# First attention of a four-stage kernel: the division of its outputs goes from VectorE to ScalarE, VectorE and GpSimd, and 44 of 64 row maxima stand ahead of the second scores, not 56

## The chip, the cores and the metric

The kernel runs on one core of one Trainium2 chip. The metric is the device time of one execution in microseconds, the median of several runs. A core has TensorE (matrix products, PE in the rows), VectorE (DVE), ScalarE (ACT), GpSimd (POOL) and SyncE (SP, which only issues transfers here). Each engine takes its instructions in the order in which they are written and waits at semaphores for the others. TensorE writes its products to PSUM, which has eight banks of 512 float32 values in each of 128 partitions.

## The reference, cut to what matters

```python
x = L0_attn_x                                    # (8, 512, 128), 16 heads of 8
x = _layernorm(x + _L0_attn_ref(x, L0_attn_W_qkv), axis=-1)
x = _layernorm(x + _L0_ffn_ref(x, ...), axis=-1)   # mixture of 32 experts and a shared one
x = _layernorm(x + _L1_attn_ref(x, ...), axis=-1)
x = _layernorm(x + _L1_ffn_ref(x, ...), axis=-1)
...
qkv = x @ W_qkv                                   # _L0_attn_ref
q, k, v = jnp.split(qkv, 3, axis=-1)
...
scores = jnp.einsum('bhnd,bhmd->bhnm', q, k) / jnp.sqrt(jnp.float32(D_MODEL))
attn = jax.nn.softmax(scores, axis=-1)
out = jnp.einsum('bhnm,bhmd->bhnd', attn, v)
```

The change touches the first attention alone, and the places in its last stretch where the work of the expert stage begins.

## The kernel before

`attention0` works through the eight batch items. An item has 16 heads and four tiles of 128 queries, so 64 **first scores**: products of bfloat16 parts of the queries with the keys (`s1`, L627), each 128 by 512 in one bank of `ps_f`. VectorE takes the negated maximum of every row of each (`reduce_max`, L780). The maxima go back into the product: half an item at a time GpSimd splits them into three bfloat16 parts (`split_max`), TensorE turns the parts (`turn_max`, L601), ScalarE copies them out of PSUM (`take_max`, L502), and SyncE writes them as extra rows into the operand `qs` (`max_rows`, L453). The **second scores** (`s2`, L683, 64 products in 32 units `u` of two) then come out of TensorE with the maximum subtracted and the keys in the partitions; ScalarE takes their exponential (L542), and TensorE multiplies by the values (`pv`, L696, one group of four column tiles for every two units). ScalarE takes the summed outputs of eight heads (`take_o`), TensorE turns them (`turn_o`, L704), and VectorE divides them by the sum that stands in an extra column (`divide`, L791 and L229). GpSimd adds x and normalises.

The stages of neighbouring items overlap. While the 32 units of second scores of item b run (a **period** below), the remaining first scores of item b and the first ones of item b+1 are interleaved, two to a unit, at 64 **turns** 0 to 63: turns below `LATE` belong to item b, the others to item b+1. Four **guests** have a turn of their own: the two turned maxima `max0`, `max1` and the two turned outputs `o0`, `o1`. Turn n stands in unit n // 2; in an odd unit a `pv` group stands between the first turn and the second. The order of a unit on TensorE is: second scores, first turn, `pv` if the unit is odd, second turn.

```python
GUEST_AT = {"max0": MT_AT[0], "max1": MT_AT[1],
            "o0": OT_AT[0], "o1": OT_AT[1]}
TURNS = [t for n in range(S1_N) for t in [g for g, at in GUEST_AT.items() if at == n] + [n]]
BANK = {t: i % FB for i, t in enumerate(TURNS)}
```

First scores and guests go round three PSUM banks (`FB = 3`) in this order. Before a turn writes, `free_bank` waits until the turn three places back in `TURNS` has been read: a score by its maximum, a turned maximum by ScalarE's copy, a turned output by the division. So a guest takes one place in the round of three. The second scores have a pair of double banks of their own, the outputs one bank.

Ahead of period 0 stands a **lead** (`units(-1, ...)`): the first scores of item 0 from turn `LATE` on, two a unit, with no second scores. From unit `EARLY_U` on each unit of it has one of 22 `early_product`s (L614, L617) in float32, which ScalarE copies (`take_early`); units without one have three products that only keep TensorE at work (`warm_up`, L592). The second scores of item 0 wait for the last copy. SyncE's queue is written out in `step`. Between the lead and period 0's transfers stand the weights of the later stages (`load_more`), and its end waits until all of the small ones have landed. GpSimd's order stands in its own `units`; `split_qk` (L292 to L304) makes the bfloat16 parts of the item after next, which SyncE writes out and reads back as `qs` and `ks` (`parts_to_dram`, `stack`). In the last period `Front` begins the routing of the experts: for seven items TensorE turns x (L950) and, two units later, multiplies it by the gate (L942), at the units `X_AT0`.

## Time and profile before

| | us |
|---|---|
| median of 3 runs | 1024.18 (1024.17 to 1026.49) |
| the profiled execution, its own time | 1023.77 |
| its span, first to last instruction | 1021.7 |
| TensorE, VectorE, ScalarE, GpSimd busy in the span | 979.9, 826.8, 732.8, 523.6 |
| from the start to the first second scores (the lead) | 51.5 |
| a period of 32 units in the middle of the first attention | 41.6 |

Times within the span are counted from its first instruction. Busy time of TensorE counts pipelined products that overlap, so 96% of the span is not 96% of what it can do. The first attention fills the span up to about 386 us.

### The profile page before, as it was taken

What the parts mean: (1) busy time and instruction counts of PE and PEld (TensorE: products, weight loads), DVE (VectorE), ACT (ScalarE), POOL (GpSimd) and SP (SyncE); (2) the same over time, 40 slices, a digit from 0 to 9 for tenths busy, and PEclk for the clock granted to TensorE, in tenths of its full rate; (3) what the DMA queues carried; (4) which work ended last, traced back from release to release, by engine and by line L of the source; (5) the groups of instructions that cost most, each with busy time, mean ns of one, the idle gap of its engine ahead of it and who ended that gap; (6) DMA issues with size and microseconds to landing.
All of it is one profiled execution on the core that took longest, in us unless ns stands there. A gap on an engine that the chain in (4) does not pass through costs nothing. (4 is left out here: it accounts for less than half of the span.)

```text
span 1021.7 us, 20122 instructions
## 1 busy us (share of the span) xinstructions
PE 979.9 (96%) x5769; PEld 469.4 (46%) x5769; DVE 826.8 (81%) x1811; ACT 732.8 (72%) x945; POOL 523.6 (51%) x631
## 2 busy tenths in 40 slices
PE   8999999999999999999999999999999999999996
PEld 4422222222222246888888887863232333222585
DVE  7999999999999867889788789987666666644677
ACT  4377887878888776655555555668889888999753
POOL 3051744726538745677677676675443144310275
PEclk9999999999999999999999999999999999999999
DMA  7661223122130005323433432443422332230011
GB/s 229 205 226 48 81 64 109 45 87 95 40 109 17 3 4 165 122 87 127 143 99 95 154 115 80 151 147 98 150 87 68 92 123 73 66 108 1 1 32 52
DMA packets 73548, 97.04 MB, mean 95 GB/s; under 512 B 12620, under 2 KB 42188, under 8 KB 73100
## 3 DMA queue, kind: packets, MB, share of 16 engines
q1 hardware_dynamic: 73496, 96.40, 29.7%
q8 instruction: 26, 0.43, 0.2%
q14 instruction: 26, 0.21, 0.1%
HBM read 68.18 MB, written 27.79 MB: 94 GB/s over the span
## 5 line engine op out<-in xcount | busy, mean ns | idle before, releaser
L780 DVE TENSOR_REDUCE a_nmax<-a_ps_f 128x1 f32<-128x512 f32 x512 | 319.7, 683 | 7.7 <-PE a_ps_f L627 5.3
L542 ACT ACTIVATE a_prob<-a_ps_s 128x1024 f32<-128x1024 f32 x256 | 250.0, 1022 | 63.5 <-PE a_ps_s L683 62.3
L1428 ACT ACTIVATE a_prob<-a_ps_s 128x1024 f32<-128x1024 f32 x256 | 244.4, 1026 | 27.8 <-PE a_ps_s L1480 26.8
L2248 POOL TENSOR_TENSOR moe_hl<-moe_hid,moe_hh 128x512 fp32r<-128x512 f32 x134 | 174.2, 1305 | 84.1 <-ACT moe_hh L2129 84.0
L627 PE MATMUL a_ps_f<-a_ks,a_qs 48*128 48x512 bf16 x512 | 156.9, 384 | 10.7 <-DVE a_nmax L780 3.1
L2119 ACT ACTIVATE moe_ps<-moe_ps 128x512 f32<-128x512 f32 x128 | 74.5, 582 | 111.6 <-PE moe_ps L2042 110.8
L1493 PE MATMUL a_ps_o<-a_prob,a_va 128*32 128x512 f32 x1024 | 136.4, 605 | 1.8 <-DVE a_turned_o L1608 1.2
L696 PE MATMUL a_ps_o<-a_prob,a_va 128*32 128x512 f32 x1024 | 136.4, 605 | 0.5 <-ACT a_prob L542 0.4
L683 PE MATMUL a_ps_s<-a_qs,a_ks 51*128 51x512 bf16 x512 | 131.8, 381 | 1.7 <-ACT a_prob L542 1.4
L627 PEld LDWEIGHTS a_ps_f<-a_ks,a_qs 48*128 48x128 bf16 x512 | 38.5, 93 | 193.9 <-DVE a_nmax L780 188.1
L2170 DVE TENSOR_TENSOR moe_prod<-moe_cw,moe_ps 128x512 f32<-128x512 f32 x128 | 87.3, 682 | 27.4 <-PE moe_ps L2042 26.7
L1480 PE MATMUL a_ps_s<-a_qs,a_ks 48*128 48x512 bf16 x512 | 91.0, 384 | 11.2 <-ACT a_prob L1428 10.0
L2179 DVE TENSOR_TENSOR moe_hid<-moe_prod,moe_ps 128x512 f32<-128x512 f32 x128 | 86.9, 679 | 6.1 <-DVE moe_prod L2170 1.9
L2129 ACT ACTIVATE moe_hh<-moe_hid 128x512 fp32r<-128x512 f32 x136 | 84.8, 624 | 6.1 <-DVE moe_hid L2179 5.9
L1480 PEld LDWEIGHTS a_ps_s<-a_qs,a_ks 48*128 48x128 bf16 x512 | 23.1, 93 | 129.1 <-ACT a_prob L1428 104.7
L838 POOL TENSOR_TENSOR a_msplit<-a_nmax,g_zero 128x32 bf16<-128x32 f32 x16 | 3.8, 239 | 142.7 <-DVE a_nmax L780 142.7
L2040 PE MATMUL moe_ps<-moe_xh,moe_whig 128*128 (+1 forms) x136 | 55.0, 405 | 1.3 <-DVE moe_hid L2179 1.3
L2067 PE MATMUL moe_ps<-moe_hl,moe_whid 128*128 128x512 f32 x136 | 53.9, 397 | 0.9 <-POOL moe_hl L2248 0.9
L2040 PE MATMUL moe_ps<-moe_xh,moe_whiu 128*128 (+1 forms) x136 | 53.8, 395 | 0.0
L2062 PE MATMUL moe_ps<-moe_hh,moe_wlod 128*128 128x512 f32 x136 | 53.7, 395 | 0.0
L2041 PE MATMUL moe_ps<-moe_xh,moe_wlog 128*128 (+1 forms) x136 | 53.7, 395 | 0.0
L2061 PE MATMUL moe_ps<-moe_hh,moe_whid 128*128 128x512 f32 x136 | 53.6, 394 | 0.0
(324 smaller groups left out, 1636.1 us busy)
## 6 DMA issues: line engine op xcount, KB each, us to landing
moe_cw<-r_weights SPq DMA_DIRECT2D x256, 128.0 KB, 2.8
parts_q<-a_parts SPq DMA_DIRECT2D x48, 256.0 KB, 2.5
parts_k<-a_parts SPq DMA_DIRECT2D x48, 256.0 KB, 2.6
a_qs<-parts_q SPq DMA_DIRECT2D x126, 96.0 KB, 2.4
a_ks<-parts_k SPq DMA_DIRECT2D x126, 96.0 KB, 2.4
out_x<-g_X SPq DMA_DIRECT2D x7, 256.0 KB, 2.3
a_prob<-in_x_t SPq DMA_DIRECT2D x3, 512.0 KB, 5.4
moe_wg<-in_wg SPq DMA_DIRECT2D x1, 1088.0 KB, 6.7
```

Source lines behind the costliest of these rows:

```text
L542: nc.scalar.activation(prob[:, u % PSLOTS, :, :], ps_s[:, u % 2, :, :], ACT.Exp, scale=float(P) ** -0.5).then_inc(exp_done, 1)
L627: nc.tensor.matmul(ps_f[:, bank, :], stack_rows(qs[p], h, QKR)[:, qt * P:(qt + 1) * P], stack_rows(ks[p], h, QKR), start=True, stop=True). ...
L683: mm = nc.tensor.matmul(ps_s[:, u % 2, i, :], stack_rows(ks[p], h, MXR)[:, kt * P:(kt + 1) * P], stack_rows(qs[p], h, MXR), start=True, st ...
L696: mm = nc.tensor.matmul(ps_o[j * CT:(j + 1) * CT, :], v_of_head(va[p], kt, grp * HG + j), prob[:, (2 * e + j // UN) % PSLOTS, j % UN, :], ...
L780: nc.vector.tensor_reduce(nmax[:, half_no, h % 2, col:col + 1], ps_f[:, bank, :], AX.X, ALU.max, negate=True).then_inc(max_done, 1)
L1428: nc.scalar.activation(prob[:, u % PSLOTS, :, :], ps_s[:, u % 2, :, :], ACT.Sigmoid, scale=float(HD) ** -0.5).then_inc(exp_done, 1)
L1480: mm = nc.tensor.matmul(ps_s[:, u % 2, i, :], stack_rows(ks[p], h, QKR)[:, kt * P:(kt + 1) * P], stack_rows(qs[p], h, QKR), start=True, st ...
L1493: mm = nc.tensor.matmul(ps_o[j * CT:(j + 1) * CT, :], v_of_head(va[p], kt, grp * HG + j), prob[:, (2 * e + j // UN) % PSLOTS, j % UN, :], ...
L2040: nc.tensor.matmul(dst, w[0][:, j, :], hi, start=True, stop=False)
L2170: nc.vector.tensor_tensor(prod[:, bank(j), :], cw[:, slot(j), :], ps_u[:, bank(j), :], ALU.mult).then_inc(prod_done, 1)
L2179: nc.vector.tensor_tensor(hid[:, hid_at(j), :], prod[:, bank(j), :], ps_g[:, bank(j), :], ALU.mult).then_inc(hid_done, 1)
L2248: nc.gpsimd.tensor_tensor(hl[:, part_at(j), :], hid[:, hid_at(j), :], hh[:, part_at(j), :], ALU.subtract).then_inc(hl_done, 1)
```

## The change

`LATE` goes from 8 to 20: the lead has 44 turns, and 20 of the 64 first scores of an item stand in its own period. The early products begin at unit 10, where the lead's first turn now is. The two turned maxima move from turns 47 and 11 to 58 and 24. For all items but the last, ScalarE copies a turned output from PSUM to `turned_o` in SBUF (`take_turned`), which frees the bank; VectorE takes the reciprocal of the sums from there at turn 50 or 13 (`invert`), and GpSimd multiplies (`divide`). GpSimd's `split_qk` moves behind the split of the maxima and behind this multiplication, SyncE's `parts_to_dram` behind `max_rows`. In the last period, turning x for the router begins at unit 13 and routing at unit 18, where they began at 7 and 14.

```diff
--- before.py
+++ after.py
@@ -51,7 +51,7 @@
 WEIGHT_SCALE = 1.0 / 127.0
 S1_N = H * NT
 FB = 3
-LATE = 8
+LATE = 20
 WARM = (5, 2, 3)
 PLACED = 2
 RC, CW_EARLY = 8, 3
@@ -60,11 +60,12 @@
 HH = H // 2
 V_AT = 16
 EARLY = [("q", 1), ("k", 1), ("v", 0), ("v", 1)] + [(name, b) for b in range(2, NB) for name in "qkv"]
-EARLY_U = 5
+EARLY_U = 10
 EARLY_BANKS = 4
-MT_AT = (47, 11)
+MT_AT = (58, 24)
 OT_AT = (46, 9)
 STATS_AT = 16
+REC_AT = (50, 13)
 LOOP_U = 11
 
 
@@ -348,6 +349,7 @@
         osb = [sb("osb0", [P, T]), e["dsb"]]
         sel = prob[:, PSLOTS - 1, :, :].rearrange("p i t -> p (i t)").bitcast(BF16)[:, 0:2 * PARTS * PLACED * (HALF + QKR)]
         sel = sel.rearrange("p (n a j m) -> p n a j m", n=2, a=PARTS, j=PLACED)
+        turned_o = sb("turned_o", [P, T])
         pool_gate, qk_gate = sb("pool_gate", [P, 1]), sb("qk_gate", [P, 4])
         squares, half_sums, sums, share = sb("squares", [P, NT, P]), sb("half_sums", [P, NT, P // 2]), sb("sums", [P, NT]), sb(
             "share", [P, NT])
@@ -376,6 +378,7 @@
         s2_done, exp_done, pv_done = sem("s2_done"), sem("exp_done"), sem("pv_done")
         o_taken, ot_done, rec_done, att_done, sum_done, norm_step = (
             sem(n) for n in ("o_taken", "ot_done", "rec_done", "att_done", "sum_done", "norm_step"))
+        o_copied = sem("o_copied")
 
 
         S2_C, EXP_C, PV_C, O_C, OT_C, ATT_C = NU, 2, PSLOTS // 2, 1, 2, 1
@@ -458,11 +461,10 @@
                     max_rows(b, p, 1)
                 if fore and back:
                     stack(b + 1, 1 - p, NG - 1, True)
-                if qk_on:
-                    parts_to_dram(b + 2, p)
                 if fore:
                     max_rows(b + 1, 1 - p, 0)
                 if qk_on:
+                    parts_to_dram(b + 2, p)
                     sp.wait_ge(parts_out, OUT_C * (b + 3) + OUT_C)
                     for grp in range(NG - 1):
                         stack(b + 2, p, grp, True)
@@ -526,6 +528,11 @@
                 act.wait_ge(ot_done, NO * b + n - 1 + OT_C)
                 take(osb[n][:, :], ps_o[:, :], pv_done, NE * b + PER_O * NT * (n + 1) + PV_C, o_taken)
 
+            def take_turned(b, n):
+
+                act.wait_ge(att_done, NO * b + n + ATT_C)
+                take(turned_o[:, :], ps_f[:, BANK[f"o{n}"], :], ot_done, NO * b + n + 1 + OT_C, o_copied)
+
             def take_max(b, half_no):
 
                 k = 2 * b + half_no
@@ -547,6 +554,10 @@
                         for t in turns_of(u, second):
                             if fore and back and t == V_AT and not is_first(b):
                                 place_v(b + 1, 1 - p)
+                            if back and t == "o0" and not is_last(b):
+                                take_turned(b, 0)
+                            if tail and t == "o1" and not is_last(b):
+                                take_turned(b - 1, 1)
                             if fore and t == "max0":
                                 take_max(b + 1, 0)
                             if back and t == "max1":
@@ -638,7 +649,11 @@
                 elif t in ("max0", "max1"):
                     pe.wait_ge(mt_copied, 2 * b + (t == "max0"))
                 else:
-                    pe.wait_ge(att_done, NO * (b - 1) + (int(t[1]) + 1) % NO + ATT_C)
+                    count = NO * (b - 1) + (int(t[1]) + 1) % NO
+                    if is_last(b - 1):
+                        pe.wait_ge(att_done, count + ATT_C)
+                    else:
+                        pe.wait_ge(o_copied, count)
 
             def take_turn(b, p, t, qk_on, fore, back, tail):
 
@@ -780,6 +795,12 @@
                 nc.vector.tensor_reduce(nmax[:, half_no, h % 2, col:col + 1], ps_f[:, bank, :], AX.X, ALU.max,
                                         negate=True).then_inc(max_done, 1)
 
+            def invert(b, n):
+
+                dve.wait_ge(o_copied, NO * b + n + 1)
+                dve.wait_ge(att_done, NO * b + n + ATT_C)
+                nc.vector.reciprocal(rec[:, :, :, :], output_parts(turned_o[:, :])[:, :, :, :, HD]).then_inc(rec_done, 1)
+
             def divide(b, n):
 
                 o = output_parts(ps_f[:, out_bank(b, n), :])
@@ -796,10 +817,14 @@
                 for u in range(u0, u1):
                     for second in range(2):
                         for t in turns_of(u, second):
-                            if back and t == "o0":
+                            if back and t == "o0" and is_last(b):
                                 divide(b, 0)
-                            if tail and t == "o1":
+                            if tail and t == "o1" and is_last(b):
                                 divide(b - 1, 1)
+                            if back and t == REC_AT[0] and not is_last(b):
+                                invert(b, 0)
+                            if tail and t == REC_AT[1] and not is_last(b):
+                                invert(b - 1, 1)
                             if isinstance(t, int) and (back if t < LATE else fore):
                                 reduce_max(*score_of(t, b), BANK[t])
                     if is_last(b):
@@ -843,6 +868,15 @@
                 pool.wait_ge(mt_chain, 3 * k + 3)
                 nc.gpsimd.tensor_tensor(msplit[:, :, 2, :], mrest[:, :, :], msplit[:, :, 1, :],
                                         ALU.subtract).then_inc(mt_parts, 1)
+
+            def divide(b, n):
+
+                o, to = output_parts(turned_o[:, :]), outputs_of(att, n)
+                pool.wait_ge(rec_done, NO * b + n + 1)
+                for q in range(PER_O):
+                    ins = nc.gpsimd.tensor_tensor(to[:, :, :, q, :], o[:, :, :, q, 0:HD],
+                                                  rec[:, :, :, q].unsqueeze(3).broadcast_to([P, NT, HG, HD]), ALU.mult)
+                ins.then_inc(att_done, 1)
 
             def add_x(b):
 
@@ -891,9 +925,11 @@
                 if u0 == 0 and is_first(b):
                     front.split_weight(pool, 0)
                 if u0 == 0 and tail:
+                    if not is_last(b):
+                        divide(b - 1, 1)
                     add_x(b - 1)
                     normalise(b - 1)
-                if u1 == NU and qk_on:
+                if u1 == NU and qk_on and not back:
                     split_qk(b + 2, 0)
                     split_qk(b + 2, 1)
                 if u1 == NU and fore:
@@ -906,6 +942,11 @@
                     if isinstance(b, int) and b < 0:
                         pool.wait_ge(x_in, 16)
                         pool.wait_ge(early_taken, len(EARLY))
+                    if back:
+                        divide(b, 0)
+                    if qk_on and back:
+                        split_qk(b + 2, 0)
+                        split_qk(b + 2, 1)
                     if isinstance(b, int) and b == NB - 2:
                         front.split_weight(pool, 3)
                         front.split_weight(pool, 4)
@@ -918,9 +959,9 @@
     return FirstOutput(nc, g, e, m, o_taken, osb[1], rec, att, ln, ot_done, rec_done, att_done, sum_done)
 
 
-X_AT0 = (7, 9, 11, 13, 21, 23, 25)
+X_AT0 = (13, 15, 17, 19, 21, 23, 25)
 X_POOL = (4, 5, 6)
-EXP_AT, ROUTE_U, CT_U = 13, 14, 23
+EXP_AT, ROUTE_U, CT_U = 18, 18, 23
 NEXT_ROUTE_AT = (26, 28, 28, 28, 29, 29, 29, 30, 30, 30, 31, 31)
 ROUTE_PER_U = 2
 
```

The order on TensorE in the first half of the loop's body, from the second scores of unit 23 on. `a_ps_s` are second scores, `a_ps_f<-a_ks,a_qs` first scores, `a_ps_o` is `pv`, `a_ps_f<-g_ident,a_osb` the guest `o0` and `a_ps_f<-a_identb,a_msplit` the guest `max0`. Before:

```order
L683 MATMUL a_ps_s<-a_qs_76,a_ks_77 128x512 x2
L637 REGISTER_ALU
L704 MATMUL a_ps_f<-g_ident,a_osb 128x128 x4
L637 REGISTER_ALU
L627 MATMUL a_ps_f<-a_ks,a_qs 128x512
L696 MATMUL a_ps_o<-a_prob,a_va_78 32x512 x4
L637 REGISTER_ALU
L600 ISA
L601 MATMUL a_ps_f<-a_identb,a_msplit 96x128
L627 MATMUL a_ps_f<-a_ks,a_qs 128x512
```

And now, the same place with `o0`, then unit 29 with `max0`:

```order
L698 MATMUL a_ps_s<-a_qs_76,a_ks_77 128x512 x2
L648 REGISTER_ALU
L719 MATMUL a_ps_f<-g_ident,a_osb 128x128 x4
L648 REGISTER_ALU
L638 MATMUL a_ps_f<-a_ks,a_qs 128x512
L711 MATMUL a_ps_o<-a_prob,a_va_78 32x512 x4
L648 REGISTER_ALU
L638 MATMUL a_ps_f<-a_ks,a_qs 128x512
...
L698 MATMUL a_ps_s<-a_qs_76,a_ks_77 128x512 x2
L648 REGISTER_ALU
L611 REGISTER_ALU
L612 MATMUL a_ps_f<-a_identb,a_msplit 96x128
L648 REGISTER_ALU
L638 MATMUL a_ps_f<-a_ks,a_qs 128x512
L711 MATMUL a_ps_o<-a_prob,a_va_78 32x512 x4
```

`o0` stays where it is. `max0` stood behind the `pv` of the same unit; now it stands in another unit, ahead of the first turn and of `pv`.

The order on TensorE around `max1`. Before, where it stands in unit 5, behind `o1` in unit 4:

```order
L704 MATMUL a_ps_f<-g_ident,moe_dsb 128x128 x4
L627 MATMUL a_ps_f<-a_ks_77,a_qs_76 128x512
L680 REGISTER_ALU
L683 MATMUL a_ps_s<-a_qs,a_ks 128x512 x2
L637 REGISTER_ALU
L627 MATMUL a_ps_f<-a_ks_77,a_qs_76 128x512
L696 MATMUL a_ps_o<-a_prob,a_va 32x512 x4
L600 REGISTER_ALU
L601 MATMUL a_ps_f<-a_identb,a_msplit 96x128
```

And now, in unit 12:

```order
L698 MATMUL a_ps_s<-a_qs,a_ks 128x512 x2
L648 REGISTER_ALU
L611 REGISTER_ALU
L612 MATMUL a_ps_f<-a_identb,a_msplit 96x128
L648 REGISTER_ALU
L638 MATMUL a_ps_f<-a_ks_77,a_qs_76 128x512
L648 REGISTER_ALU
L638 MATMUL a_ps_f<-a_ks_77,a_qs_76 128x512
L695 REGISTER_ALU
L698 MATMUL a_ps_s<-a_qs,a_ks 128x512 x2
L650 REGISTER_ALU
L638 MATMUL a_ps_f<-a_ks_77,a_qs_76 128x512
```

It stands alone now, three first scores ahead of the next `pv`, and the first score behind the next unit's second scores has its bank.

On VectorE the division in the first half of the body was, and is now:

```order
L780 TENSOR_REDUCE a_nmax<-a_ps_f 128x1
L786 REGISTER_ALU
L788 REGISTER_ALU
L791 RECIPROCAL a_rec<-a_ps_f 128x32
L229 TENSOR_TENSOR moe_y<-a_ps_f,a_rec 128x4x32 x2
```

```order
L795 TENSOR_REDUCE a_nmax<-a_ps_f 128x1
L800 REGISTER_ALU
L802 RECIPROCAL a_rec<-a_turned_o 128x32
L794 REGISTER_ALU
L795 TENSOR_REDUCE a_nmax<-a_ps_f 128x1
```

The two multiplications are gone from VectorE, and the reciprocal stands four maxima later.

## Rows read from the trace of the kernel before

**Rows 1.** The page: busy time of each engine.

```profile
PE 979.9 (96%) x5769; PEld 469.4 (46%) x5769; DVE 826.8 (81%) x1811; ACT 732.8 (72%) x945; POOL 523.6 (51%) x631
```

**Rows 2.** One period: length; busy PE, PEld, DVE, ACT, POOL; clock, DMA share, GB/s.

```profile
176.70:218.30 41.60, 40.21 (x266) 10.11 (x266) 41.17 (x71) 33.28 (x38) 22.14 (x43) 1.00 0.25 77
```

**Rows 3.** Waits, 176.7 to 260 us: in total, times, longest.

```profile
PEld a_ps_f L627 <- DVE a_nmax L780: 48.9, 89, 0.8
...
DVE a_nmax L780 <- PE a_ps_f L627: 0.6, 2, 0.3
```

**Rows 4.** Timeline of VectorE: start, length; maxima 1, 4 and 5 of five.

```profile
210.44 0.69 DVE L780 TENSOR_REDUCE a_nmax<-a_ps_f 128x1 f32<-128x512 f32 x1
...
212.24 0.68 DVE L780 TENSOR_REDUCE a_nmax<-a_ps_f 128x1 f32<-128x512 f32 x1
...
212.93 0.69 DVE L780 TENSOR_REDUCE a_nmax<-a_ps_f 128x1 f32<-128x512 f32 x1
```

**Rows 5.** Timeline of TensorE in the same two units.

```profile
211.18 0.09 PEld L627 LDWEIGHTS a_ps_f<-a_ks,a_qs 48*128 48x128 bf16 x1 [0.51 <-DVE a_nmax L780]
...
211.50 1.07 PE L696 MATMUL a_ps_o<-a_prob,a_va 128*32 128x512 f32 x8
...
212.50 0.39 PE L627 MATMUL a_ps_f<-a_ks,a_qs 48*128 48x512 bf16 x1
```

**Rows 6.** Timeline around `o0`: TensorE, VectorE; two exponentials of ScalarE.

```profile
205.42 0.66 PE L704 MATMUL a_ps_f<-g_ident,a_osb 128*128 128x128 f32 x4
...
206.48 0.35 DVE L791 RECIPROCAL a_rec<-a_ps_f 128x32 f32<-128x32 f32 x1
206.86 0.49 DVE L229 TENSOR_TENSOR moe_y<-a_ps_f,a_rec 128x128 f32<-128x128 f32 x2
207.26 11.93 DVE L780 TENSOR_REDUCE a_nmax<-a_ps_f 128x1 f32<-128x512 f32 x19
...
213.22 1.94 ACT L542 ACTIVATE a_prob<-a_ps_s 128x1024 f32<-128x1024 f32 x2 [0.55 <-PE a_ps_s L683]
```

**Rows 7.** Timeline of VectorE at a period's start.

```profile
179.02 3.77 DVE L780 TENSOR_REDUCE a_nmax<-a_ps_f 128x1 f32<-128x512 f32 x6 [0.30 <-PE a_ps_f L627]
```

**Rows 8.** Timeline of the lead: TensorE; last early copy on ScalarE.

```profile
13.01 0.82 PE L592 MATMUL a_ps_o<-a_identb 128*128 128x512 bf16 x3
...
14.85 1.13 PE L617 MATMUL a_ps_s<-a_xt,a_w 128*128 128x512 f32 x2
...
45.78 0.60 ACT L520 ACTIVATE a_early_v<-a_ps_s 128x512 f32<-128x512 f32 x1 [0.81 <-PE a_ps_s L614]
...
51.51 0.39 PE L683 MATMUL a_ps_s<-a_qs,a_ks 51*128 51x512 bf16 x2
```

**Rows 9.** Timeline of period 0: copy and transfer of maxima; next period's first exponential.

```profile
59.44 0.27 ACT L502 ACTIVATE a_mparts<-a_ps_f 96x128 bf16<-96x128 bf16 x1 [0.60 <-PE a_ps_f L601]
...
64.49 1.49 SPq L453 DMA_DIRECT2D a_qs<-a_mparts  x2
...
93.11 1.02 ACT L542 ACTIVATE a_prob<-a_ps_s 128x1024 f32<-128x1024 f32 x1 [0.55 <-PE a_ps_s L683]
```

**Rows 10.** DMA issues on the page: median us to landing.

```profile
a_qs<-parts_q SPq DMA_DIRECT2D x126, 96.0 KB, 2.4
```

**Rows 11.** Timeline of TensorE in the last period: second scores of units 8, 10, 28.

```profile
352.52 0.70 PE L683 MATMUL a_ps_s<-a_qs,a_ks 51*128 51x512 bf16 x4
...
355.62 0.61 PE L683 MATMUL a_ps_s<-a_qs,a_ks 51*128 51x512 bf16 x4
...
380.43 0.61 PE L683 MATMUL a_ps_s<-a_qs,a_ks 51*128 51x512 bf16 x4
```

**Rows 12.** GpSimd by form, 176.7 to 218.3 us; timeline of GpSimd and SyncE.

```profile
L200 POOL TENSOR_TENSOR a_half_sums<-a_half_sums 128x128 f32<-128x128 f32 x2 | 0.9, 462 | 0.2
...
196.32 0.20 POOL L295 TENSOR_TENSOR a_qk_gate<-g_zero 128x1 f32<-128x1 f32 x1
...
206.15 0.87 SPq L263 DMA_DIRECT2D parts_k<-a_parts  x2
```

## The prediction

> **What bounds the kernel now.** I read the page first, for the engines: TensorE seems full and VectorE comes next [rows 1], but TensorE's records overlap, so this decides nothing. The busy times of one middle period say that VectorE is at work for 41.17 of 41.60 us [rows 2]. The waits say nearly the same from the other side: the first scores wait 48.9 us for maxima in two periods, the maxima 0.6 us for scores [rows 3]. So far VectorE is the bound, and whatever leaves it is a gain.
>
> The timeline, maximum by maximum, says something else. From 210.44 to 212.24 us three maxima start 0.60 us apart; the next starts 0.69 later [rows 4]. This fourth one is the turn behind `pv`: its score starts at 212.50 and its maximum at 212.93, 0.43 behind, which is the bare way from product to maximum. VectorE could have begun at 212.84 and waits 0.09, too little for the views to call idle. Following the chain back: the maximum that starts at 210.44 ends at 211.13, the score three places on loads its weights at 211.18, having waited for it (this is the bank), `pv` stands behind that score and starts at 211.50, and the next score can start when its 1.00 us is over, at 212.50 [rows 4, 5]. The loop is 0.69 + 0.05 + 0.32 + 1.00 + 0.43 = 2.49 us, and four turns take 2.49 us. So three PSUM banks, and `pv` in TensorE's order, set the pace; VectorE would need 4 x 0.60 = 2.41. It has 0.08 us to spare in four turns and nothing more.
>
> A rule that speaks against the change goes with this. By the Trainium skill, Perfetto Trace Analysis, section Optimization Strategy, the same small gap repeated on the engine that should be saturated can mean that there is too little PSUM for the next tile; the repeated 0.08 us is such a gap. It would put the gain of a lighter VectorE at that gap alone; my sum comes out the same way from the loop.
>
> A period of 64 turns is then 16 x 2.485 = 39.76. The two divisions with the guests beside them bring it to 41.6: a division holds VectorE from 206.48 to 207.26, 0.78 [rows 6], and the period's start idles 0.30 [rows 7]; 39.76 + 2 x 0.78 + 0.30 = 41.62.
>
> **The change, part by part.** All is counted against the profiled execution, 1023.77 us (0.4 below the median of 1024.18).
>
> *The lead.* Before, a unit with three warming products stands ahead of the first early product: they start at 13.01, the product at 14.85. Now the product takes the place at 13.01, 1.84 earlier; 22 units with a product follow as before, with one turned maximum among them. The last copy ends at 46.38 before [rows 8], so now at 44.54, and the second scores may start at 44.6 where they started at 51.51: **-6.9**. The turned maximum is no later than that: it stands two products before the end, and its transfer needs two issues of 0.75 and a landing of 2.4 [rows 9, 10], about 4.2 in all against 4.1 of products and 0.7 of copy.
>
> *A guest alone.* Here the change costs. A guest takes one place in the round of three banks. With `o0` ahead of the turn before `pv`, that turn gets the bank of the score two back instead of three, whose maximum starts one pitch later: the loop grows by 0.60. Before, this lay under the division (0.78) and `max0` stood in the same four turns, as did `max1` beside `o1`: two guests, one stall. Now the four stand in four places. `max0` at turn 58 has the same place as `o0`, ahead of the score before `pv`: +0.60. `max1` at turn 24 stands three scores ahead of `pv`; the score before `pv` gets the bank of `max1` itself, which ScalarE frees. ScalarE comes to it only behind the exponential of unit 12. That exponential starts 0.72 behind the score after `pv` (213.22 against 212.50), two take 1.94, of which the first holds ScalarE for 0.92 [rows 5, 6], and the copy takes 0.27 [rows 9]. Counted from the score after `pv`, the bank is free at 1.91, where the maximum of the score three places back would have freed it at 0.43 + 0.69 + 0.05 = 1.17. The loop grows by the 0.74 between them and by the 0.05 of a release: **0.79**. Bounds: a guest costs nothing if VectorE has scores in store (its place in the order, 0.2 of TensorE, is what would remain), and 0.78 by the division's row.
>
> *The divisions.* VectorE now does the reciprocal alone: 206.48 to 206.86, 0.38 [rows 6], less the 0.08 to spare: 0.30, at a turn of its own. The guest's 0.60 now stands bare. Together 0.90 each where a division was 0.79. ScalarE's two copies, of 0.60 each as in [rows 8], fit: in 2.49 us it has two exponentials of 1.94, and the copy lies behind the exponential and before the bank is asked for. If the cover is gone, a copy's 0.60 is paid. GpSimd's two multiplications are 0.46 each by its row of this size [rows 12], 1.0 at most.
>
> *A middle period* is then 39.76 + 2 x 0.90 + 0.79 + 0.60 + 0.30 = 43.25, against 41.64: +1.61, six times: **+9.7**.
>
> *Period 0.* From the second scores to those of period 1 it was 93.11 - 0.72 - 51.51 = 40.9 [rows 8, 9]. Now, without `o1`: 39.76 + 0.90 + 0.79 + 0.60, less 0.5 since there is no `pv` in the first cycle: 41.5, **+0.6**. And a new wait. The maxima of the second half are copied at 59.7 but their transfer is issued at 64.49 [rows 9], since SyncE waits for the weights of later stages to land. That was hidden: unit 16, the first to need them, came half a period after 51.51, near 72. Now it is due eight cycles after 44.6, less 0.5 and with the 0.79 of `max1`, at 64.8. The weights are queued behind the lead's turned maximum, which comes 1.84 earlier by the start and 1.4 later by one more product; I take them 0.5 earlier. The transfer then begins at about 64.0, its second half at 64.75, and by the 2.4 of a transfer eight times as large [rows 10] it lands at 67.1 at the latest; I take 66.6. TensorE stands in front of unit 16 with the first scores behind it: **+1.8** (bounds 0, if the weights land 2 us earlier, and 2.3).
>
> *The queues.* GpSimd's order: `split_max` for turn 51, the division, then `split_qk`, from 196.32 until SyncE writes its last part at 206.15, 9.8 us [rows 12]. Maxima are ready about 36 us into a period, so the parts are ready at 48.2, that is 4.9 in the next; written (three issues of 0.44 and a landing of 2.4, 3.7) and read back (four issues, 3.8 with the landing of the last) [rows 10, 12] by 12.4, where the first score of the item is due at 13.9. A margin of 1.5 us, with the multiplications at 1.0 still 0.4. Cost nothing.
>
> *The last period.* Units 0 to 9 now have first scores, so unit 10 comes 0.4 later (a single guest's 0.60 less what the older order lost). Before, two clusters of turned x stood in it; a pair of units with one takes 355.62 - 352.52 = 3.10, about 3.0 with the next ones. From unit 10 to unit 28 it was 24.8 [rows 11]. Now unit 10 to 14 has little (2 x 1.94 of exponentials at least, 4.6 with a turned maximum and a turned x), then come seven pairs of 3.0 to 3.1, `o0` adding 0.6, one of them: 4.6 + 7 x 3.06 + 0.6 = 26.6. +1.8 and +0.4, and 0.3 for routing that starts closer to its exponential: **+2.5**.
>
> Sum: -6.9 + 9.7 + 0.6 + 1.8 + 2.5 = +7.7, so **1031.5 us**. Its own range, by guests at 0.45 to 0.8 (27 places): 1027 to 1035.
>
> **The rivals.** A measurement of this kernel can tell about 0.3%, 3.1 us, from no change.
>
> *VectorE is the bound after all.* 41.17 of 41.60 us busy [rows 2] speak for it, the 0.69 step in every fourth place [rows 4] against it. Then a guest costs nothing, each of 13 divisions saves 0.78 - 0.38 = 0.40, together 5.2, the lead 6.9, and the last period and unit 16 take back 2.5 and 1.8: 1016.0, **faster**. It decides if the guests cost less than 0.1 each. The Trainium skill states the rule behind it, Perfetto Trace Analysis, Identifying the Most-Contended Engine: for VectorE occupancy is a fair measure, and the engine with the highest is to be optimised first. Chance 0.25.
>
> *Guests cost half.* Scores stored in other banks hide part: 27 places of 0.25 less give about 1025. Chance 0.10.
>
> *The parts of the next item come late.* If writing and reading back take over 1.5 us more than in rows 10, each later microsecond is paid in six periods: 1 us late is 1037. Chance 0.06.
>
> My forecast has 0.59, of which 0.04 lies within 0.3%.
>
> **The numbers.** Faster 0.25, within 0.3% 0.13, slower 0.62. The range reaches from 1015 to 1036; below it a part of the first rival is left out, above it the third.
>
> **What the profile of the changed kernel would show.** The first second scores at about 44.6. A middle period of 43.2. Steps of 1.2 to 1.3 us from one maximum to the next, with idle of 0.5 to 0.7 put down to the first scores, at turns 11, 27, 47 and 59, and none before. A transfer of maxima at about 64 in period 0 with TensorE idle until 66.5. No wait of first scores for parts. I am wrong if the four turns with a guest alone take 2.5 us, or if a middle period is below 41.6.

## The result, and the profile after

The changed kernel takes **1031.11 us** (median of 4 runs, 1030.48 to 1031.7), the kernel before 1024.3 us beside it: a ratio of 1.0056, with an interval of 1.0036 to 1.0075. It is slower by 6.8 us, where +7.7 was forecast; the time itself lies 0.4 us from the forecast and inside its range. The profiled execution took 1030.48 us, its span is 1028.6.

One middle period, which answers to [rows 2], with the same columns:

```profile
174.48:217.36 42.88, 40.79 (x268) 10.53 (x268) 40.20 (x68) 33.89 (x39) 23.68 (x48) 1.00 0.23 75
```

It is longer by 1.28 us while VectorE works 0.97 us less in it. What stands in its way shows in the waits from 174.48 to 260.24 us (two periods, as in [rows 3]; total, times, longest):

```profile
PEld a_ps_f L638 <- DVE a_nmax L795: 47.5, 80, 0.8
...
DVE a_nmax L795 <- PE a_ps_f L638: 5.3, 10, 0.6
```

The maxima waited 0.6 us for scores, now 5.3. The page has the same for the whole span: the group of the maxima with its idle time behind the second bar, before and after.

```profile
L780 DVE TENSOR_REDUCE a_nmax<-a_ps_f 128x1 f32<-128x512 f32 x512 | 319.7, 683 | 7.7 <-PE a_ps_f L627 5.3
```

```profile
L795 DVE TENSOR_REDUCE a_nmax<-a_ps_f 128x1 f32<-128x512 f32 x512 | 319.5, 683 | 25.8 <-PE a_ps_f L638 23.9
```

The timeline of VectorE in that period says where (start, length, work, count, idle before it):

```profile
182.84 1.29 DVE L795 TENSOR_REDUCE a_nmax<-a_ps_f 128x1 f32<-128x512 f32 x2 [0.60 <-PE a_ps_f L638]
184.05 0.34 DVE L802 RECIPROCAL a_rec<-a_turned_o 128x32 f32<-128x32 f32 x1
184.31 8.11 DVE L795 TENSOR_REDUCE a_nmax<-a_ps_f 128x1 f32<-128x512 f32 x13
...
193.68 12.43 DVE L795 TENSOR_REDUCE a_nmax<-a_ps_f 128x1 f32<-128x512 f32 x20 [0.62 <-PE a_ps_f L638]
206.71 1.89 DVE L795 TENSOR_REDUCE a_nmax<-a_ps_f 128x1 f32<-128x512 f32 x3 [0.60 <-PE a_ps_f L638]
208.51 0.34 DVE L802 RECIPROCAL a_rec<-a_turned_o 128x32 f32<-128x32 f32 x1
...
214.87 2.48 DVE L795 TENSOR_REDUCE a_nmax<-a_ps_f 128x1 f32<-128x512 f32 x4 [0.60 <-PE a_ps_f L638]
```

Four stops of 0.6 us: ahead of the maxima of turns 11 (182.84), 27 (193.68), 47 (206.71) and 59 (214.87). Between them stand the two reciprocals. Below I call the time from the start of the maximum of turn 4k-1 to that of turn 4k+3 **cycle** 4k+3. It takes 2.49 us where nothing disturbs it. I read the sixteen cycles of each period off VectorE's timeline, for this kernel and all that follow; each ends with the first maximum behind a `pv`. A period is counted from the maximum of one turn 63 to the next.

| us | before | after |
|---|---|---|
| cycle 3 (the period's start) | 2.79 | 2.79 |
| cycle 11, 15 (`o1`, its reciprocal) | 3.27, 2.49 | 3.08, 2.60 |
| cycle 27 (`max1` now) | 2.49 | 3.27 |
| cycle 47, 51 (`o0`, its reciprocal) | 3.28, 2.49 | 3.08, 2.61 |
| cycle 59 (`max0` now) | 2.49 | 3.08 |
| maximum of turn 63, period 0 | 92.81 | 88.71 |
| the same, period 6 | 342.86 | 346.41 |
| first product of the expert stage | 385.69 | 391.75 |

The lead gives what was asked of it. The second scores begin here (TensorE):

```profile
45.11 0.39 PE L698 MATMUL a_ps_s<-a_qs,a_ks 51*128 51x512 bf16 x2 [0.73 <-issue]
```

And the wait of unit 16 in period 0, forecast as new, is there. ScalarE has copied the maxima at 62.05, but SyncE waits for the small weights and issues them at 64.35; TensorE waits for them until 67.57. The first line is from the waits of SyncE from 38 to 70 us (L2591 is the end of `load_more`), the others from the timeline.

```profile
SPq L2591 <- DMA a_ob<-in_o_b: 6.8, 1, 6.8
...
64.35 1.50 SPq L456 DMA_DIRECT2D a_qs<-a_mparts  x2
...
67.57 0.39 PE L698 MATMUL a_ps_s<-a_qs,a_ks 51*128 51x512 bf16 x2 [1.27 <-DMA a_qs<-a_mparts]
```

Something that the forecast left out stands in period 6, where cycle 59 is 3.58. GpSimd splits two weights of the expert stage ahead of the maxima, and comes to the maxima at 340.68, 0.5 us too late for turn 58:

```profile
332.14 4.81 POOL L1074 TENSOR_TENSOR moe_wlog<-moe_wg,moe_whig 128x2176 fp32r<-128x2176 f32 x1
336.91 3.81 POOL L1071 TENSOR_TENSOR moe_whiu<-moe_wu,g_zero 128x2176 fp32r<-128x2176 f32 x1
340.68 0.23 POOL L863 TENSOR_TENSOR a_msplit<-a_nmax,g_zero 128x32 bf16<-128x32 f32 x1
```

### The profile page after: what moved, and what is told of

Read it like the earlier page. It is cut to its first block and busy times, and to the rows that moved or that the text cites. A ratio compares the mean times of both kernels' runs of the same rounds, so it can differ in the third digit from the quotient of the medians.

```text
span 1028.6 us, 20103 instructions
## 1 busy us (share of the span) xinstructions
PE 979.0 (95%) x5751; PEld 470.4 (46%) x5751; DVE 821.8 (80%) x1785; ACT 736.3 (72%) x958; POOL 534.0 (52%) x657
## 3 DMA queue, kind: packets, MB, share of 16 engines
q1 hardware_dynamic: 73496, 96.40, 29.9%
## 5 line engine op out<-in xcount | busy, mean ns | idle before, releaser
L795 DVE TENSOR_REDUCE a_nmax<-a_ps_f 128x1 f32<-128x512 f32 x512 | 319.5, 683 | 25.8 <-PE a_ps_f L638 23.9
L1469 ACT ACTIVATE a_prob<-a_ps_s 128x1024 f32<-128x1024 f32 x256 | 244.5, 1026 | 28.2 <-PE a_ps_s L1521 27.1
L2289 POOL TENSOR_TENSOR moe_hl<-moe_hid,moe_hh 128x512 fp32r<-128x512 f32 x134 | 174.4, 1306 | 84.0 <-ACT moe_hh L2170 83.9
L638 PE MATMUL a_ps_f<-a_ks,a_qs 48*128 48x512 bf16 x512 | 161.0, 384 | 13.5 <-DVE a_nmax L795 3.5
L2083 PE MATMUL moe_ps<-moe_xl,moe_whig 128*128 (+1 forms) x136 | 53.6, 394 | 0.0
```

Source lines behind the costliest of these rows:

```text
L638: nc.tensor.matmul(ps_f[:, bank, :], stack_rows(qs[p], h, QKR)[:, qt * P:(qt + 1) * P], stack_rows(ks[p], h, QKR), start=True, stop=True). ...
L795: nc.vector.tensor_reduce(nmax[:, half_no, h % 2, col:col + 1], ps_f[:, bank, :], AX.X, ALU.max, negate=True).then_inc(max_done, 1)
L1469: nc.scalar.activation(prob[:, u % PSLOTS, :, :], ps_s[:, u % 2, :, :], ACT.Sigmoid, scale=float(HD) ** -0.5).then_inc(exp_done, 1)
L2289: nc.gpsimd.tensor_tensor(hl[:, part_at(j), :], hid[:, hid_at(j), :], hh[:, part_at(j), :], ALU.subtract).then_inc(hl_done, 1)
```

## The experiments

My theory: three PSUM banks and `pv` set the pace, so the price of a guest is its place in the round, 0.60 us ahead of `pv` and nearly nothing behind it, and taking the division off VectorE is worth nothing by itself. The rival: VectorE is the bound. In the table, **period** is a middle one, **expert** the first product of the expert stage, both from the profile; the ratio is to the kernel before, run beside it (median 1023.77 to 1024.3), with its interval. Profile and median are not of the same execution: for division_alone and maxima_behind_pv the profiled one is 3.5 and 2.5 us above the median, for best and all_behind_ve 2.2 and 3.1 below.

| kernel | median, us | ratio | period, us | expert, us |
|---|---|---|---|---|
| before | 1024.3 | | 41.65 | 385.69 |
| the change | 1031.11 | 1.0056 (1.0036 to 1.0075) | 42.88 | 391.75 |
| division_alone | 1054.92 | 1.029 (1.0273 to 1.0308) | 46.3 to 47.3 | 419.99 |
| order_alone | 1030.08 | 1.0052 (1.0033 to 1.007) | 42.86 | 390.65 |
| place_before_pv | 1026.28 | 1.0014 (1.0004 to 1.0024) | 41.96 | 387.60 |
| place_behind_pv | 1021.75 | 0.9976 (0.9964 to 0.9987) | 41.37 | 383.44 |
| maxima_behind_pv | 1028.24 | 1.0028 (1.0012 to 1.0044) | 41.86 | 392.18 |
| late_wait | 1029.23 | 1.0047 (1.0032 to 1.0061) | 41.86 | 390.18 |
| best (all combined) | 1027.06 | 1.0024 (1.0013 to 1.0034) | 41.57 | 386.18 |
| division_max55 | 1026.57 | 1.003 (1.002 to 1.004) | 41.86 | 387.74 |
| weights_behind | 1028.82 | 1.0041 (1.0025 to 1.0057) | 41.56 | 390.56 |
| all_behind | 1026.06 | 1.0021 (1.0013 to 1.003) | 41.56 | 387.42 |
| all_behind_ve | 1030.66 | 1.0068 (1.0053 to 1.0082) | 42.51 | 389.53 |
| pairs | 1025.07 | 1.0007 (0.9997 to 1.0016) | 42.1 | 386.46 |

### The order without the new division

The change, with the division back on VectorE and all else as it is there.

```diff
-                            if back and t == "o0" and is_last(b):
+                            if back and t == "o0":
                                 divide(b, 0)
...
-                            if back and t == REC_AT[0] and not is_last(b):
-                                invert(b, 0)
...
```

(ScalarE's copies and GpSimd's multiplications go too.)

> The changed kernel with the division back on VectorE (reciprocal and both multiplications from PSUM at turns 46 and 9). If banks set the pace: the cycles with a turned output are 3.19 to 3.27 instead of 3.08 with 0.12 for the reciprocal in the next, so a middle period is 42.8 to 43.1 (42.88 in the changed kernel) and the time is that of the changed kernel within 1.5 us. If VectorE is the bound: 5 us slower than the changed kernel, 1036.

Measured: 1030.08 us, within 1.1 us of the change. Its VectorE, in the same place as above:

```profile
193.13 11.84 DVE L787 TENSOR_REDUCE a_nmax<-a_ps_f 128x1 f32<-128x512 f32 x19 [0.62 <-PE a_ps_f L634]
204.88 0.35 DVE L804 RECIPROCAL a_rec<-a_ps_f 128x32 f32<-128x32 f32 x1
205.26 0.49 DVE L230 TENSOR_TENSOR moe_y<-a_ps_f,a_rec 128x128 f32<-128x128 f32 x2
205.67 8.05 DVE L787 TENSOR_REDUCE a_nmax<-a_ps_f 128x1 f32<-128x512 f32 x13
214.31 3.18 DVE L787 TENSOR_REDUCE a_nmax<-a_ps_f 128x1 f32<-128x512 f32 x5 [0.60 <-PE a_ps_f L634]
```

The stops at turns 27 and 59 are there. At turn 47 the division stands where the stop was: the cycle is 3.19, and 3.08 + 2.61 - 2.49 = 3.20 with the new form. Its 0.79 and the stop with the reciprocal cost the same. VectorE is busy for 41.26 us of this period of 42.86, and for 40.20 of 42.88 in the change: 1.06 us less work, and no time gained. So the division moved off VectorE gains nothing in this order, and the periods are longer by the order alone. The rival falls here.

### An empty place in the round

The kernel before, with a fifth guest that does nothing but take a bank's place, ahead of `pv` (turn 30) or behind it (turn 31).

```diff
-            "o0": OT_AT[0], "o1": OT_AT[1]}
+            "o0": OT_AT[0], "o1": OT_AT[1], "none": NONE_AT}
...
+                if t == "none":
+                    return
```

> The kernel before with one more guest at turn 30 that does nothing: no engine has an instruction for it, it only takes a place in the round of three banks, ahead of the score before pv. If banks set the pace: the cycle of turns 28 to 31 is 3.08 us instead of 2.49; since 69 places divide by three, the break of the round at the period's start goes, and with it 0.30; a middle period is 41.95, seven times +0.3: 2 us slower. If it is VectorE, or the work of a guest, nothing changes at turn 31.

> The same empty guest at turn 31, behind pv. If banks set the pace: the score behind pv and the next three have a bank in time, the cycle stays at 2.49, and only the break of the round at the period's start goes: the step at turn 3 falls from 0.98 to 0.68, a middle period is 41.35, 2 us faster than before. If VectorE is the bound, no difference to the kernel with the empty guest at turn 30.

Measured: 1026.28 and 1021.75 us. VectorE with the empty guest at turn 30:

```profile
226.09 13.71 DVE L785 TENSOR_REDUCE a_nmax<-a_ps_f 128x1 f32<-128x512 f32 x22
240.40 9.35 DVE L785 TENSOR_REDUCE a_nmax<-a_ps_f 128x1 f32<-128x512 f32 x15 [0.60 <-PE a_ps_f L630]
```

And at turn 31, through turn 31 and through the start of the next period at 258.10:

```profile
223.70 23.06 DVE L785 TENSOR_REDUCE a_nmax<-a_ps_f 128x1 f32<-128x512 f32 x37
...
247.47 15.00 DVE L785 TENSOR_REDUCE a_nmax<-a_ps_f 128x1 f32<-128x512 f32 x24
```

No work is added, only the bank of later turns changes. Ahead of `pv` the place costs its cycle 0.59; behind `pv` nothing at all. Both take away the 0.30 at a period's start [rows 7]: 64 turns and four guests are 68 places, which three banks don't divide, and with 69 the round closes with the period. The kernel with the place behind `pv` is the fastest of this study, below the kernel before by 0.24%: seven starts of a period by 0.30 are 2.1 us, and it is 2.45 below the 1024.20 beside it.

### The maxima behind pv, and SyncE's wait moved

The change with the turned maxima at turns 55 and 23; then also with SyncE's wait for the small weights behind its loop; then ("best") also with the empty guest at turn 31.

```diff
-MT_AT = (58, 24)
+MT_AT = (55, 23)
...
+            m["small_in"](sp)
             step(NB - 2, 0, False, True, True)
...
+            def small_in(sp):
                 sp.wait_ge(moe_in, 2 * 16)
                 sp.wait_ge(c1_in, 8 * 16)
```

> The changed kernel with the turned maxima at turns 55 and 23, behind pv, in place of 58 and 24. Bank theory: their cycles cost 0.2 instead of 0.60 and 0.79, a middle period is 41.9 to 42.0 instead of 42.88, seven times: 6 to 7 us faster than the changed kernel, about 1024.5. Rival (each guest alone costs what its own work and ScalarE's copy cost, wherever it stands): no gain.

> As the one with the turned maxima behind pv, and SyncE waits for the small weights of the later stages behind its loop instead of ahead of it. If the stop at unit 16 of period 0 is SyncE waiting for them: the cycle of turns 32 to 35 of period 0 is 2.5 us instead of 3.7, 1.2 us faster. Rival: the transfer of the maxima itself is late in the queues behind the weights, then the stop stays.

> As the one before, with the empty guest at turn 31. Bank theory: the break of the round goes, a middle period is 41.6 and the kernel 1021 to 1022, faster than both kernels by 0.2 to 0.3% and 1%. Rival: the maxima's transfer, which must land by the period's start, takes the 0.3 back.

The middle periods do as expected: cycles 23 and 55 are 2.67, cycles 27 and 59 are 2.49, a period 41.86, and 41.57 with the empty guest (one of them is 42.07, with a cycle 23 of 3.18). The sums missed, 1028.24, 1029.23 and 1027.06, for two reasons that the middle periods don't have.

Period 6 took 46.54, 46.28 and 45.30 us. GpSimd's order there, in the first of the three:

```profile
328.99 4.82 POOL L1074 TENSOR_TENSOR moe_wlog<-moe_wg,moe_whig 128x2176 fp32r<-128x2176 f32 x1
333.76 3.82 POOL L1071 TENSOR_TENSOR moe_whiu<-moe_wu,g_zero 128x2176 fp32r<-128x2176 f32 x1
337.53 0.24 POOL L863 TENSOR_TENSOR a_msplit<-a_nmax,g_zero 128x32 bf16<-128x32 f32 x1
```

With `max0` at turn 55, three turns earlier, the same two weights hold it up by 2.85 us (cycle 55 is 5.52, 2.67 in the other periods). The cycle behind it is 3.79, with TensorE at the lower of its two clocks from 338.6 us on (0.50 granted from 340 to 343).

Period 0 (its sixteen cycles) took 46.1, 44.6 and 42.6. TensorE's granted clock tells the first two from the third. The second, then the third of the kernels, with the columns of [rows 2]:

```profile
46.00:50.00 4.00, 3.44 (x21) 0.64 (x17) 3.90 (x7) 3.71 (x4) 0.00 (x0) 0.94 0.95 325
50.00:56.00 6.00, 5.65 (x27) 0.99 (x23) 3.57 (x7) 2.24 (x3) 0.00 (x0) 0.50 0.89 368
```

```profile
46.00:50.00 4.00, 3.44 (x23) 0.74 (x18) 3.70 (x7) 3.81 (x4) 0.00 (x0) 1.00 0.89 297
50.00:56.00 6.00, 5.30 (x40) 1.14 (x36) 5.40 (x9) 3.99 (x4) 0.00 (x0) 1.00 0.97 395
```

That is a difference of executions as much as of kernels: the twelve of "best" took 1024.25 to 1028.61 us at mean granted clocks of 0.996 down to 0.991, and the profiled one, 1024.83, is the third fastest. Not even the fastest is below the 1024.11 of the kernel before.

Whether the moved wait of SyncE does what it was for: cycle 35 of period 0 is 3.68 with the change and 2.49 here, but 2.49 also without the move, where slow cycles before it had given the transfer its time. With the clock up, in "best", it is 2.49 too. SyncE's queue tells more. In the change the maxima are copied at 62.05 and issued 2.30 us later. In the last kernel of this document (pairs), which has the move, they are copied at 62.14 and issued at once:

```profile
62.17 1.50 SPq L466 DMA_DIRECT2D a_qs<-a_mparts  x2
```

Unit 16 then starts at 66.84 without a wait, and cycle 35 is 2.49. In order_alone, which like pairs has the division on VectorE but not the move, the same copy ends at 62.02, the issue comes at 63.86 and cycle 35 is 3.22. So SyncE's wait was the stall, and not a transfer late behind the weights. What the move is worth in the whole is not shown alone.

### The new division without the order

The kernel before with the new division, and nothing else.

```diff
-LATE = 20
+LATE = 8
...
-MT_AT = (58, 24)
+MT_AT = (47, 11)
...
-                if u1 == NU and qk_on and not back:
+                if u1 == NU and qk_on:
```

(Shown against the changed kernel; `EARLY_U`, `X_AT0` and the places of the routing, GpSimd's place for `split_qk` and SyncE's order are as before too.)

> The kernel before with the new division alone: ScalarE copies the turned outputs, VectorE keeps the reciprocal, GpSimd multiplies; 56 maxima in the lead and both turned maxima at turns 47 and 11 as before. If the round of three banks sets the pace, the cycle of four turns with two guests (turned outputs 0.60, turned maxima behind pv 0.19) stays at 3.27 us without the division on VectorE, the reciprocal adds 0.12 in two other cycles, and a middle period is 41.65 to 41.9: the same time or up to 1.7 us more. If VectorE is the bound, each of 13 divisions saves 0.40 us or more, a period is 40.8 and the kernel 5 us faster.

Measured: 1054.92 us, which neither theory had. Cycles 11 and 15 are 3.27 and 2.60, as expected. But cycle 47 is 5.7 to 7.0 and cycle 51 is 3.4 to 3.8 from period 1 on. The waits of TensorE from 96.25 to 377.16 us (six periods) name the turned maxima behind GpSimd:

```profile
PE a_ps_f L613 <- POOL a_msplit L870: 19.2, 6, 3.4
```

GpSimd's timeline in one period: maxima of the second half, the multiplication for `o1`, the last step of `split_qk`, maxima of the first half.

```profile
149.19 0.24 POOL L864 TENSOR_TENSOR a_msplit<-a_nmax,g_zero 128x32 bf16<-128x32 f32 x1 [14.35 <-DVE a_nmax L796]
...
153.31 0.78 POOL L878 TENSOR_TENSOR moe_y<-a_turned_o,a_rec 128x128 f32<-128x128 f32 x2 [2.92 <-DVE a_rec L803]
...
175.44 1.15 POOL L305 TENSOR_TENSOR a_parts<-a_rest,a_parts 128x512 bf16<-128x512 f32 x1
176.55 0.24 POOL L864 TENSOR_TENSOR a_msplit<-a_nmax,g_zero 128x32 bf16<-128x32 f32 x1
```

The kernel before, in its own:

```profile
140.52 0.24 POOL L838 TENSOR_TENSOR a_msplit<-a_nmax,g_zero 128x32 bf16<-128x32 f32 x1 [16.66 <-DVE a_nmax L780]
...
142.01 1.27 POOL L850 TENSOR_TENSOR moe_y<-moe_y,g_X 128x512 f32<-128x512 f32 x1 [0.28 <-DVE moe_y L229]
...
164.41 0.24 POOL L838 TENSOR_TENSOR a_msplit<-a_nmax,g_zero 128x32 bf16<-128x32 f32 x1
```

From the one split to the other it was 23.9 us with no idle time at its end, now it is 27.4: 2.9 of waiting for a reciprocal at turn 13 and 0.8 of multiplication, in a queue that had none to give. TensorE stops for it from 174.4 to 177.8 us, and works at half the clock behind it, until 184 us (columns of [rows 2]):

```profile
172.00:174.00 2.00, 1.91 (x16) 0.67 (x13) 2.00 (x4) 2.00 (x3) 1.92 (x3) 1.00 0.68 227
...
176.00:177.00 1.00, 0.00 (x0) 0.00 (x0) 0.00 (x0) 0.00 (x0) 0.92 (x3) 1.00 0.00 0
...
178.00:180.00 2.00, 2.00 (x9) 0.57 (x8) 1.28 (x3) 1.05 (x2) 0.00 (x0) 0.50 0.93 317
```

That GpSimd's queue is the cause was then tested by itself, with `max0` alone at turn 55 (against division_alone):

```diff
-MT_AT = (47, 11)
+MT_AT = (55, 11)
```

> The division on three engines with everything else as before cost 31 us, and its trace shows the first wait of each period at the turned maximum of turn 47: GpSimd's order holds it up, since the multiplication for o1 waits for a reciprocal at turn 13 and stands ahead of the layer norm, the splitting of q and k and the splitting of the maxima. Here that turned maximum alone goes from turn 47 to turn 55. If GpSimd's queue is the whole cause, the cycles of 7.0 and 3.8 us go to 2.6 or 3.1, a middle period is 39.76 + 0.30 + 0.79 + 0.11 + 0.60 + 0.12 + 0.18 = 41.86 us, and the kernel takes about 1026 us. If the copies on ScalarE or the lower clock of TensorE are a cause of their own, it stays above 1040 us.

Measured: 1026.57 us, a period of 41.86. 28 us are gone with one number. With nothing held up, the new division still leaves a period 0.21 us above the 41.65 of before, about its two reciprocals, and gains nothing. So the multiplication on GpSimd needs a later `max0`, and a later `max0` costs 0.18 behind `pv` (turn 55) where the change pays 0.60 ahead of it (turn 58).

### What is left when the guests stand right

The combined version, with GpSimd's two weights behind the maxima of period 6; then also the turned outputs behind `pv`; then that with the division on VectorE.

```diff
-                    if isinstance(b, int) and b == NB - 2:
-                        pool.wait_ge(ln["x_done"], NB - 1)
-                        pool.wait_ge(v_taken, NB)
-                        front.split_weight(pool, 1)
-                        front.split_weight(pool, 2)
                     split_max(b + 1, 0)
...
                     if isinstance(b, int) and b == NB - 2:
+                        pool.wait_ge(ln["x_done"], NB - 1)
+                        pool.wait_ge(v_taken, NB)
+                        front.split_weight(pool, 1)
+                        front.split_weight(pool, 2)
```

```diff
-OT_AT = (46, 9)
+OT_AT = (47, 11)
...
-REC_AT = (50, 13)
+REC_AT = (51, 15)
```

> The combined version spends 45.30 us in period 6 where the middle periods take 41.57, because GpSimd splits two weights of 8.6 us ahead of the maxima for turn 55. Here these two stand behind the maxima and the division. By this cause period 6 goes to 41.6 us and the kernel to 3.7 us less than the combined version: 1020.5 to 1023.5 us. If the later weights are then missed by the mixture of experts, the 3.7 us come back there and the time stays near 1027 us.

> As weights_behind, and both turned outputs go behind pv too (turns 47 and 11 in place of 46 and 9), with the reciprocals at turns 51 and 15. If the round of three banks sets the price of a guest, then each of the four guests costs what one behind pv costs (0.18 us) and each reciprocal 0.12: a middle period of 39.76 + 0.72 + 0.24 = 40.7 us in place of 41.57, and the kernel 6 us below weights_behind: 1014.5 to 1017.5 us. By the rival (VectorE is the bound, the place of a guest is nothing) it stays within 1 us of weights_behind.

> As all_behind, but VectorE does the divisions. With no bank in the way a division should cost its 0.78 less the 0.08 that VectorE has to spare, 0.70, where the other form pays 0.18 + 0.12 = 0.30: a middle period of 39.76 + 2 x 0.70 + 2 x 0.18 = 41.5 us, and 5 us more than all_behind in the whole. So the division moved off VectorE would be worth something once the guests stand behind pv. If the two are within 1 us, moving the division is worth nothing in any order.

Moving the weights: period 6 went from 45.30 to 41.69, and the last period from 45.4 to 50.4. There TensorE now waits for the other half of the maxima, behind the same weights:

```profile
PE a_ps_f L616 <- POOL a_msplit L875: 3.9, 1, 3.9
```

The wait was moved, not removed: of the two outcomes expected the second, though it is the maxima and not the mixture of experts that pay. (The profiled execution lost about 3.4 us more to the clock in period 0.)

Turned outputs behind `pv`: a period of 41.56, not 40.7, and 1026.06 us, not 1014.5 to 1017.5. A miss, and it corrects my theory. TensorE around `o0` at turn 47, then VectorE there and at turn 55:

```profile
199.27 1.06 PE L717 MATMUL a_ps_o<-a_prob,a_va 128*32 128x512 f32 x8
200.27 0.66 PE L725 MATMUL a_ps_f<-g_ident,a_osb 128*128 128x128 f32 x4
200.86 0.39 PE L642 MATMUL a_ps_f<-a_ks,a_qs 48*128 48x512 bf16 x1
```

```profile
201.28 2.48 DVE L801 TENSOR_REDUCE a_nmax<-a_ps_f 128x1 f32<-128x512 f32 x4 [0.59 <-PE a_ps_f L642]
...
206.55 8.75 DVE L801 TENSOR_REDUCE a_nmax<-a_ps_f 128x1 f32<-128x512 f32 x14 [0.20 <-PE a_ps_f L642]
```

Behind `pv` a guest stands in the loop with its own time on TensorE: 0.59 for the four products of an output (200.27 to 200.86), 0.18 for the one of a maximum, 0 for the empty one. Ahead of `pv`, at the turn before it, it costs 0.60 whatever it does. I had taken the 0.18 of a maximum for any guest. In period 0, where `o1` does nothing but has its place, the two can be told apart: with `o1` at turn 9 cycle 11 is 3.08, at turn 11 it is 2.48.

With the division on VectorE and the outputs behind `pv` (all_behind_ve) cycles 11 and 47 are 3.64 and 3.71, a period is 42.51, and the kernel takes 4.6 us more by the medians. There the division stands in the loop behind the 0.59. Moved off VectorE it is worth 0.95 us a period in this order, and nothing with `o0` at 46. The profiled executions lie only 1.5 us apart: all_behind is 5.4 us ahead at the maximum of turn 63 of period 6 (336.31 against 341.75), and gives 3.3 of it back in the last period (51.1 us against 47.8): TensorE waits 3.5 us there behind GpSimd's weights, against 2.8, and the lower clock follows only in all_behind.

### Pairs

The last try for a faster kernel: early second scores, division on VectorE, `o0` and `max0` as a pair at turns 58 and 59, `max1` at 23, the empty guest.

```diff
-MT_AT = (58, 24)
-OT_AT = (46, 9)
+MT_AT = (59, 23)
+OT_AT = (58, 9)
+NONE_AT = 31
```

> The early second scores of the change (LATE 20), the divisions on VectorE, the wait for small weights behind SyncE's loop, an empty guest behind pv at turn 31, and guests in pairs or behind pv: o0 at turn 58 ahead of the score before pv with max0 at 59 behind it, max1 at 23 behind pv, o1 alone at 9; in the last period o0 stays at turn 46. By the round of three banks the pair costs 0.79, o1 alone 0.70 and max1 0.18: a middle period of 39.76 + 1.67 = 41.43 us, no stall for GpSimd in period 6. Against the version with one empty guest and nothing else (1021.75 us) the lead gives 5.9 us, the first cycle of period 0 takes back 1.1, the periods 0.4 and the last period 2.7: about 1020 us, between 1018.5 and 1022, the upper part where TensorE's clock is lower at the first second scores. If the last period takes back 5 us or more, it stays at 1022 or above, and the early second scores are worth nothing.

Measured: 1025.07 us, above the range expected and not to be told from the kernel before (its interval holds 1). The guests cost as expected (cycle 59 3.27, 11 3.19, 23 2.67, and 47 none), but each period's start has 0.6 to 0.7 that was to be gone. From 87.84 to 340.4 us:

```profile
PE a_ps_s L703 <- DMA a_qs<-a_mparts: 4.4, 6, 0.8
```

One turn after the change's place, the maxima of the first half land up to 0.8 us after the next period wants them. That is the other bound on `max0`. At turn 58 (the change) cycle 3 is 2.79 as before, but nothing is to spare there: the second scores of period 1 start at 88.81, 0.52 behind turn 63's score, where before both start at 92.39. In the change and in pairs alike they start 3.25 us behind the issue of their maxima (85.56 and 88.81, 85.33 and 88.59).

## Why the prediction was right, by its own steps

| term | predicted | measured |
|---|---|---|
| lead | -6.9 | -6.4 (51.51 to 45.11) |
| period 0, from the first second scores | +2.4 | +2.3 (41.30 to 43.60) |
| periods 1 to 6 | +9.7 | +7.65 |
| last period | +2.5 | +2.52 |
| after the expert stage began | 0 | +0.8 |
| span | +7.7 | +6.9 |

That the time lies 0.4 us from the forecast is partly luck: the forecast starts from the profiled execution, 1023.77, and the kernel before took 1024.3 beside the change. The difference was +7.7 by the sum and +6.8 by the medians, and one of its terms is off by 2 us, with others off the other way.

**The loop of banks** held: 2.49 a cycle, +0.60 forecast for `max0` at turn 58 and 0.59 measured, +0.79 for `max1` at 24 and 0.78 measured, and +0.59 for `o0` and `o1` standing bare. order_alone and the empty guests show it apart from VectorE's work. By the Trainium skill's Perfetto Trace Analysis, Optimization Strategy, a small gap that repeats can mean that there is too little PSUM. By the empty guests the trace agrees for the 0.08 in four turns: a place that does nothing costs 0.59.

**The reciprocals** were mis-sized: 0.30 each, measured 0.12. I took the 0.38 from its start to the next instruction, but that one needs its result. A maximum starts 0.26 after it (184.05 to 184.31), and the one behind that 0.54 later and not 0.60; so VectorE is held for 0.20, of which 0.08 was to spare. Twelve of them by 0.18 are 2.2 us; with the 0.5 of the next point that is 1.7 of the 2.05 by which the six periods fell short of the sum. Another 0.2 lies in the kernel before, whose six periods took 250.05 us and not 6 x 41.64.

**GpSimd's weights** in period 6 were left out: +0.5 in cycle 59 (3.58).

**Period 0** came out by errors that cancel. The stall of unit 16 was 1.2, not 1.8, inside its bounds: the transfer landed at 67.5, 0.4 after what I had called the latest, but TensorE came to it only at 66.3, where I had 64.8. And I gave `o1` no price where it does no work; its place costs 0.59 all the same. The 0.5 that I took off has another reason than the one I gave. The first cycle, counted from the first second scores, is 2.42 in both kernels, 0.07 shorter than the others. The rest was the end of my count: 93.11 - 0.72 is the start of turn 63's score, beside which the next second scores started before. In the change they start 0.52 behind it, so by my own count, from second scores to second scores, period 0 took 43.70 against 40.88, +2.8 and not +2.4.

**The lead** was 0.5 too good: ScalarE's last early copy ends at 45.02, where I had 44.54. Its first copy starts 1.89 us earlier than before (14.12 against 16.01), as forecast, its last only 1.36 (44.42 against 45.78); what takes the difference in between is open.

**The last period**, +2.52, was a sum from pairs of units and came out to 0.02, by luck. By the starts of the second scores, up to unit 10 it lost 0.2 and not 0.4 (13.18 to 13.35), from there to unit 28 2.35 and not 1.8 (24.81 to 27.16), and behind unit 28 nothing, where I had 0.3 for the routing.

**The 0.8 after the expert stage began** (636.04 to 636.89 us) is open. All kernels of this study have 636.0 to 636.9 there.

**The rivals.** VectorE as the bound: order_alone answers it. The Trainium skill's Perfetto Trace Analysis, Identifying the Most-Contended Engine, takes VectorE's occupancy as a fair measure and would have the fullest engine optimised first. That occupancy is 41.17 of 41.60 us in [rows 2], but with the order fixed, 1.06 us less work on VectorE left the period as it was (42.86 and 42.88). Here the measurement decides against the rule: the busy time hides a wait of 0.09 that comes back in every fourth maximum. Guests at half price: refuted by the cycles. Late parts: the waits of the changed kernel from 45 to 390 us name no first score that waits for parts.

## What to carry to other kernels

When buffers go round in a fixed order, everything that takes a place in it has a price, and where the place is decides it: right ahead of the long instruction in the loop it costs a whole pitch, the time from one maximum to the next, whatever it does (an empty one too), behind it only its own time. Count the places in a round against the period: one empty place that made 68 into 69 was the only edit here that beat the kernel before. And before a helper engine gets work, look whether its queue has idle time at the end that someone waits for; GpSimd was busy half of the span and had none.

## What the runs showed of the hardware

TensorE's clock was a cost of the experiments that I had not reckoned with. Its two levels here are 1.00 and 0.50 of the granted clock, 2.4 and 1.2 GHz. In maxima_behind_pv, late_wait and weights_behind it went to the lower one between 48 and 50 us, 3 to 4 us after the first second scores, and came back 7 to 10 us later; period 0 was longer by 2.0 to 3.5 us than in the profiled execution of best, where it stayed up. TensorE's busy time from 46 to 50 us was the same in late_wait and best, 3.44 (the rows above); what decides it isn't shown. It is not the kernel alone: the kernel before, too, had executions of 1026 to 1027 us at mean clocks of 0.993 to 0.995 beside those of 1024 at 0.998. In division_alone it fell behind the stop at the turned maximum: GpSimd was late by 3.5 us (the split 33.4 us into the period, 29.9 before), TensorE stood still for 3.4, and the period was about 5 us longer. The stops of 2.5 to 3.9 us behind GpSimd in period 6 and the last period, in maxima_behind_pv, best and weights_behind, were followed by the lower clock too, but one of 2.8 us in all_behind_ve was not. So a stall can cost more than its length, and a sum like mine leaves that out: the stalls of 0.6 to 1.3 us in the change left the clock at 1.00 in the profiled execution.
